# Four sequences through Mamba, attention, FFN and a routed FFN on one core: the input norms of sequences 2 and 3 start later, the prologue waits for one load at a time, and the first scan goes ahead of the first norm's scaling

## The reference, cut to what matters

```python
x = L0_attn_x                                    # (4, 512, 128)
x = x + _L0_attn_ref(_layernorm(x), ...)         # Mamba block, then attention and a gated FFN
x = x + _L0_ffn_ref(_layernorm(x), ...)          # ternary weights, gelu, layernorm
x = x + _L1_attn_ref(_layernorm(x), ...)         # second Mamba block
x = x + _L1_ffn_ref(_layernorm(x), ...)          # eight experts, the best one for each token
...
def mamba_block(x, ...):
    xz = rmsnorm(x, norm_m_w) @ in_proj_w.T
    x_ssm, z = jnp.split(xz, 2, axis=-1)
    x_ssm = silu(causal_conv(x_ssm, conv_w, 4 taps) + conv_b)
    Bp, Cp, dt_raw = split(x_ssm @ x_proj_w.T)
    delta = softplus(dt_raw @ dt_w.T + dt_b)
    # h = exp(delta * A) * h + delta * B * x ;  y = sum(h * C)   over 16 states
    y = selective_scan(x_ssm, delta, A, Bp, Cp, D_skip) * silu(z)
    return residual + y @ out_proj_w.T
```

## Time and profile before

| what | before |
|---|---|
| median of 3 runs, us | 734.0 (730.71 to 735.45) |
| profiled execution, us | 736.92 |
| its span, us | 735.1 |
| busy share of the span: PE, DVE, ACT, POOL | 81%, 80%, 67%, 57% |
| TensorE clock granted, mean | 0.919 of full |

### The profile page before, as it was taken

How to read it: one execution, slowest core, us unless ns; L and a number is a source line. 1 busy time by engine, 2 the same in 40 slices (tenths; PEclk the granted TensorE clock), 3 DMA queues, 4 the chain that set the end, 5 groups by cost and what they waited for, 6 DMA issues and landing times. The chain is left out here.

```text
span 735.1 us, 9892 instructions
## 1 busy us (share of the span) xinstructions
PE 596.1 (81%) x3364; PEld 395.2 (54%) x3364; DVE 587.0 (80%) x592; ACT 495.3 (67%) x921; POOL 420.3 (57%) x234
## 2 busy tenths in 40 slices
PE   6686686888988969998698996898677677869995
PEld 2154363456554545545454554554444466659995
DVE  3599989998989759987697889788899899854442
ACT  3859834877598786897878789678966678313231
POOL 0078754555666464735566346675687567445663
PEclk9689879798999889999899997899899899989999
DMA  4670650075005700007400075003800751257771
GB/s 133 261 238 15 238 223 1 0 282 195 25 4 193 284 0 2 1 2 290 186 1 0 1 266 210 1 0 101 361 1 1 263 199 53 67 162 236 220 228 42
DMA packets 35661, 91.63 MB, mean 125 GB/s; under 512 B 7492, under 2 KB 13115, under 8 KB 35611
## 3 DMA queue, kind: packets, MB, share of 16 engines
q1 hardware_dynamic: 34138, 87.93, 34.1%
q0 software_dynamic: 1472, 3.06, 1.5%
HBM read 87.87 MB, written 3.11 MB: 124 GB/s over the span
## 5 line engine op out<-in xcount | busy, mean ns | idle before, releaser
L527 POOL TENSOR_TENSOR hc<-hst,bc 128x1024 f32<-128x1024 f32 x127 | 299.0, 2362 | 164.6 <-DVE hst L1096 78.8
L1108 DVE TENSOR_TENSOR_SCAN hst<-dA,bank 128x1024 f32<-128x1024 f32 x84 | 191.4, 2282 | 2.1 <-PE bank L1760 0.2
L671 ACT ACTIVATE dA<-delta,m_A_s 128x511 f32<-128x511 f32 x256 | 173.2, 712 | 9.1 <-DVE hst L1108 6.0
L1470 PE MATMUL bank<-ident,hc 128*128 128x128 f32 x1016 | 142.8, 289 | 12.8 <-POOL hc L527 12.7
L1470 PEld LDWEIGHTS bank<-ident,hc 128*128 128x128 f32 x1016 | 125.3, 151 | 42.9 <-issue 24.0
L1079 DVE TENSOR_TENSOR bank<-bank,bc 128x1024 f32<-128x1024 f32 x79 | 97.1, 1229 | 10.0 <-DMA bc<-crows 3.7
L1377 PE MATMUL bank<-arena 128*32 128x128 f32 (+6 forms) x466 | 52.6, 361 | 11.9 <-ACT arena L761 6.5
L467 POOL TENSOR_TENSOR du<-delta,xs 128x512 f32<-128x512 f32 x15 | 19.1, 1273 | 71.5 <-DVE delta L1120 71.5
L1096 DVE TENSOR_TENSOR_SCAN hst<-dA,bank 128x512 f32<-128x512 f32 x44 | 53.7, 1220 | 1.5
L1090 DVE TENSOR_TENSOR_SCAN hst<-dA,bank 128x512 f32<-128x512 f32 x44 | 53.5, 1215 | 0.8
L1377 PEld LDWEIGHTS bank<-arena 128*32 128x32 f32 (+3 forms) x466 | 26.5, 141 | 38.9 <-issue 21.5
(11 more groups left out here) (262 smaller groups left out, 1092.8 us busy)
## 6 DMA issues: line engine op xcount, KB each, us to landing
bc<-crows SPq DMA_DIRECT2D x126, 512.0 KB, 9.3
bc<-in_w SPq DMA_DIRECT2D x23, 512.0 KB, 4.0
xin<-in_xT SPq DMA_DIRECT2D x8, 256.0 KB, 4.4
rows_out<-arena SPq DMA_DIRECT2D x1, 1056.0 KB, 6.4
conv<-in_m_cw SPq DMA_DIRECT2D x2, 512.0 KB, 4.5
crows<-prow SPq DMA_DIRECT2D x8, 64.0 KB, 1.6
arena<-rows_out,source POOLq DMA_INDIRECT x23, 3.5
out_rows<-zs,target POOLq DMA_INDIRECT x23
```

The lines of the kernel that those rows point to most:

```text
L527: pool.tensor_tensor(hc[:, g % HCRING], hst[:, g % HRING], bc[:, p, 1], ALU.mult) \
L671: act.activation(dA[:, g % RING, j, 1:], delta[:, h, 1:], ACT.Exp, scale=M[mamba_of(c)]["A"][:, h, n:n + 1]).then_inc(sems["dA"], 1)
L1108: dve.tensor_tensor_scan(hst[:, g % HRING].rearrange(flat), dA[:, g % RING].rearrange(flat), bank[:, first_bank:first_bank + 2, :].rearran ...
L1470: last = pe.matmul(bank[:, YB, P * j:P * j + P], hc[:, g % HCRING, n, P * j:P * j + P], ident[:], start=False, stop=s % PAIRS == PAIRS - 1 ...
```

## The change

Three things. In the **prologue**, `mean_d` gets a semaphore of its own, so that `n_center(0)` waits for the input and `center`, and only `n_variance(0)` for `mean_d`; the two copies of C rows on ScalarE go behind both decays of step 0; the root for the layernorm of sequence 0 moves into the loop (slot 0 of block 0) and the scaling of the z weights to slot 1, both behind the diagonal matrices. The **first scan**: `n_scaled` moves from slot 1 (ahead of `scan(0)`) to slot 3 (ahead of `scan(1)`). The **norms**: sequence 2 starts at slot 26 of block 0 (where sequence 3 was), sequence 3 at slot 34, which is slot 2 of block 1.

```diff
-NSTART = {1: 2, 2: 14, 3: 26}
+NSTART = {1: 2, 2: 26, 3: 34}
+N_SCALED = 3
+ROOT_AT = 0
+WZ_AT = 1
...
-            for dst, src in first:
-                sp.dma_start(dst, src).then_inc(sems["first_loaded"], 16)
+            sp.dma_start(center[:], d["center"]).then_inc(sems["first_loaded"], 16)
+            sp.dma_start(mean_d[:], d["mean_d"]).then_inc(sems["taps_in"], 16)
...
             def beside(b, t):
+                if b == 0 and t == ROOT_AT:
+                    inverse_root(bank[:, TB7, :], ht[:], eps_ln, "n_var", 1, "n_log", "n_rs")
+                if b == 0 and t == WZ_AT:
+                    act.activation(M[0]["wz"][:], M[0]["wz"][:], ACT.Copy, scale=norm_m[:]).then_inc(sems["scaled"], 1)
...
                     for k, at in NSTART.items():
-                        if b == 0:
-                            norm_ahead(k, t - at)
+                        norm_ahead(k, 32 * b + t - at)
...
                     decay(g, j)
-                    if g == 0:
+                if g == 0:
+                    for j in range(2):
                         act.wait_ge(sems["setup_pe"], 3 + j)
                         act.activation(bc[:, 0, 1, j], bank[:, (YB, FB5)[j], :], ACT.Copy).then_inc(sems["setup_act"], 1)
-            inverse_root(bank[:, TB7, :], ht[:], eps_ln, "n_var", 1, "n_log", "n_rs")
             act.wait_ge(sems["second_loaded"], 16 * len(second))
-            act.activation(M[0]["wz"][:], M[0]["wz"][:], ACT.Copy, scale=norm_m[:]).then_inc(sems["scaled"], 1)
             diagonal(0)
...
-                    if b == 0 and t == 1:
+                    if b == 0 and t == N_SCALED:
                         n_scaled()
...
-            pe.wait_ge(sems["first_loaded"], 16 * len(first))
+            pe.wait_ge(sems["first_loaded"], 16)
             n_center(0)
             warm(1)
+            pe.wait_ge(sems["taps_in"], 16)
             n_variance(0)
```

More of the change, by code:

```diff
@@ L339, in streams @@
                     yield "attention", i, a
-        first = [(dst[:], d[key]) for dst, key in ((center, "center"), (mean_d, "mean_d"))]
         def weights_of(m):
@@ L491, in weights @@
                     pool.wait_ge(sems["late_loaded"], 16 * len(late))
-                    pool.wait_ge(sems["taps_in"], 16)
+                    pool.wait_ge(sems["taps_in"], 32)
                     pool.tensor_tensor(conv[:], conv[:], winx1[:].unsqueeze(1).to_broadcast([P, TAPS, HALVES * P]),
@@ L499, in beside @@
                     for k, at in NSTART.items():
-                        if b == 0 and t == at + NAT["xn"]:
+                        if 32 * b + t == at + NAT["xn"]:
                             n_input(k)
@@ L1789, in beside @@
                     for k, at in NSTART.items():
-                        if b == 0 and t == at + NAT["cen"]:
+                        if 32 * b + t == at + NAT["cen"]:
                             n_center(k)
-                        if b == 0 and t == at + NAT["var"]:
+                        if 32 * b + t == at + NAT["var"]:
                             n_variance(k)
```

## The result

| | before | after |
|---|---|---|
| median of 20 runs each, us | 735.54 (730.71 to 741.54) | 738.91 (733.77 to 743.19) |
| profiled execution, span, us | 736.92, 735.1 | 738.95, 737.2 |
| TensorE clock granted, mean of that execution | 0.919 | 0.912 |

The ratio is 1.0055, 95% interval 1.0037 to 1.0074: the changed kernel is some 3 to 4 us slower, where 0.5 us less was forecast. That the median of 738.91 lies inside the stated range of 729 to 739, by 0.1 us, is luck: before itself came out at 735.54, where the three runs that the forecast had gave 734.0.

What follows compares the result with a forecast made beforehand. It took the prologue and ScalarE's queue to bound the first 36 us, block 1's preparation the rest of block 0. Terms -2.2 + 0 - 0.2 + 1.9 + 0 = -0.5 us took 734.0 to 733.5, range 729 to 739.

Steps and rivals of the forecast that it cites:

- The prologue: Start of the kernel: without mean_d in its wait, sequence 0's centring starts earlier, -2.2 us, bounds 0 and -2.25.
- the first rival: Prologue: center lands with mean_d, so nothing is gained there and block 1's added matmul costs; 736.0 us, chance 0.2.
- the third rival: Prologue: TensorE's clock rises too late for the earlier matmuls, up to 3.5 us more; 737.0 us, chance 0.1.
- ScalarE's order and the early scan: Block 0's start: second scan 1.65 us earlier, lost in later waits; 0 on the chain, bounds 0 and -1.65.
- The second rival: Block 0: VectorE's lead of 1.65 us reaches the end of the block; 731.9 us, chance 0.15.
- The third sequence's norm: Middle of block 0: sequence 2's norm leaves, only the y copy ahead of 64.84 profits; -0.2 us, bounds 0 and -0.5.
- SyncE: SyncE's queue: block 1's rows leave 3.3 us later, 1.5 us of cover left; 0, at most +1.
- the fourth rival: Head of block 1: SyncE's rows come late and the first drives wait, +1.5 us; 735 us, chance 0.05.
- The fourth sequence's norm at the head of block 1: Sequence 3's centring between accumulate(14) and accumulate(15) on the chain: +1.9 us, bounds +0.9 and +2.1; its variance matmul hidden.
- What is gained or lost before 98 us is then carried unchanged: Behind 98 us: no further gain or loss, as VectorE has no idle time from 97.53 through block 1's weight preparation.
- clock effects down the line that no row shows: Later blocks: named as what could move the time by over 1%, 7.3 us; no term in the sum.

Runs made afterwards that it cites:

- the two with the dummy: Kernel before plus one unread centring matmul between accumulate(14) and accumulate(15), compared twice against before: ratios 1.0050 and 1.0058.
- the one with the norms alone: Kernel before with only sequence 2's norm moved to slot 26 and sequence 3's to slot 34: 746.61 us, ratio 1.0069 against before.
- the two with the third norm back: Changed kernel with sequence 2's norm back at slot 14, sequence 3's at slot 34 or at 36: ratios 0.9993 and 1.0004 against before.
- the three comparisons: Changed kernel with all its parts against the kernel before, measured three times: ratios 1.0055, 1.0025 and 1.0013.
- half: Kernel before plus an unread 128x256 matmul between accumulate(14) and accumulate(15): 736.23 us, ratio 0.9957 against before.
- Before once more: Kernel before, unchanged, profiled a second time: span 732.0 us, 3.1 less than the profile that the forecast rests on.

## Why the prediction was wrong, by its own steps

**The prologue: over-sized by the one execution it was read from.** The load was right: `center` had landed by 3.7, so the first rival's condition, that it lands with `mean_d`, is false. Of the -2.2, the profiled pair shows 0.74 at the first decay (24.96 to 24.22), because the first projection ran at the low clock; that was the third rival, at about a third of its price of 3.5 us, and it happened in 2 of the 11 profiles with the own semaphore. The larger error is another. In the nine profiles of kernels with the common semaphore the centring began between 4.11 and 5.79, with a median of 4.58, with the own one between 3.41 and 3.88. The profile of before that I had was the latest of all. Medians of the first delta are 22.86 and 22.09, so the term is -0.8.

**ScalarE's order and the early scan: right, as far as the runs can tell.** 0 forecast, ratio 0.9998. VectorE waited 1.12 us for the softplus at 32.10, as the step had it. The second rival, that the lead of 1.65 us carries, is not borne out: from the first delta to the gate that kernel took 72.72 us, the two profiles of before 73.34 and 72.66. The interval of its ratio (0.9971 to 1.0025) by itself would allow it.

**The third sequence's norm: agrees in one pair, not shown.** The delta of block 1 moved by -0.93, which is the -0.74 that was left of the prologue and the -0.2 of this term. But from the first delta to that one the two profiles of before took 58.84 and 58.16 us, and the three of the changed kernel 58.66, 58.00 and 58.57, so 0.2 is under what these profiles can tell.

**SyncE: right.** The rows left 2.4 us later and released no drive; the fourth rival is false.

**The fourth sequence's norm at the head of block 1: right in place, wrong in price.** The matmul took the forecast 1.9 us in the chain, `n_variance(3)` was hidden (the residual at 104.98 had no wait), and the head grew by 0.8 to 1.1 in the seven profiles that have the whole matmul there, less than 1.9, since the clock rises behind it. The gate stood at 97.69, inside the 95.5 to 98.5 that the forecast allowed. At the end the same matmul costs 4.1 us against before (744.91 to 740.79) and 4.9 against the same matmul two slots later.

**The step that failed** is the last of the sum: "What is gained or lost before 98 us is then carried unchanged". Taken up to the gate, the measured terms cancel: -0.8 for the prologue and +0.8 to +1.1 for the head. The profiled pair says the same (+0.16 us at the gate, -0.36 at 174 us, +2.1 at the end). The loss comes behind 98 us, where the forecast had none. VectorE has indeed no idle time up to the weight preparation, but TensorE's clock down the line is not fixed: summed from the granted clocks of 5 us stretches it was at the low level for some 116 us in the profile of before and 126 in the changed one. The reading that fits best is that a shift by one microsecond moves the later idle times of TensorE against the clock's changes, and a stretch at the low level ends before or behind work that others wait for. With the whole matmul in the chain all seven profiles had the long follow-up (76.3 to 76.7 us), and the runs lean the same way: the clock was under 0.915 in 17 of 20 runs of the changed kernel (6 of 11 and 4 of 12 in its later comparisons, whose ratios were lower too) and in 9 of 9, 10 of 12 and 11 of 12 of the two with the dummy and the one with the norms alone, against 8 of 35, 12 of 29, 10 of 33, 5 of 32 and 4 of 23 for before in the five groups. A low clock alone does not make a kernel slow, though: the two with the third norm back had it in 9 of 12 and 9 of 11 runs, with ratios of 0.9993 and 1.0004. Within before's own runs a clock lower by 0.01 goes with 3 to 5 us more (lines through the runs of each group), so the 0.01 that separates 0.920 from 0.910 is of the size of what the head does not explain. That the clock is the cause and not a fellow of the longer time is argued from the matmuls themselves (1.90 against 2.92 to 3.63 us for one projection that others wait for) and not shown, since no run set the clock by hand. The forecast named "clock effects down the line that no row shows" and used them for the range alone, with no rival and no chance of their own.

**The sum, with measured terms:** -0.8 + 0 - 0.2 + 4.1 = +3.1 us, beside the +3.4, +1.5 and +1.9 of the three comparisons, as medians. The 4.1 is the price of the unread matmul in before and already holds what follows behind 98 us; with the third norm back the same place did not cost it, so the sum is near the first comparison and no proof. The forecast's own bounds add up to -3.5 and +3.6, where it has -3.4 and +3.5.

The Trainium skill (TensorE: Matmul & The Clock Gate, section on what's actually happening) says that the number of slow matmuls differs from run to run of one kernel and that the ramp costs less than 1% of a typical span. The first agrees with the two profiles of before, with 107 and 116 us at the low level. The second is said of the ramp; this kernel goes down and up all along, and the 20 runs of before spread over 1.5%.

**What stays open.** What decides between the two patterns was not found. It isn't the length in the chain (whole 1.0058, half 0.9957), nor the start of the block (the gate stood at 95.05 and 94.66 in good ones, at 94.64 in a poor one). Why the centring in the chain costs nothing when the third norm is back (0.9993), and why that norm's return gains nothing when the fourth is off the chain (1.0004 where 0.998 and less was expected), stays open; the parts of this change don't add up.

## What to carry to other kernels

A wait that one execution shows for a load is a sample: take its spread from a second profile of the same kernel before you sell the whole of it. Where TensorE goes between its two clock levels all the time, a matmul of 1.9 us put into the chain cost four and one of 1.06 gave three to four back, so a forecast from summed durations has to leave room of a few times its terms, with a chance for each side. Put a side task behind the last matmul that others wait for, not between two of them: two slots later the same norm cost nothing that could be measured. And judge such an edit by many runs: one program's profiles differed here by 2 us in one follow-up and by 2.7 us in one block.

## What the runs showed of the hardware

- Before once more against before: equal programs, spans 732.0 and 735.1 us, TensorE busy 591.7 and 596.1 us up to 730 us. The clock was at the low level for some 107 and 116 us of that time, summed from the granted clocks of 5 us stretches.
- Two loads of 64 KB, issued 0.47 us apart on one queue: the first released the centring between 3.41 and 3.88 in the eleven profiles where it stands alone, both together between 4.11 and 5.79 in nine.
- The same program, twice: 58.77 and 61.47 us from the first delta to the delta of block 1, with a granted clock of 1.00 and of 0.50 from 64 to 66 us.
- An added matmul of 1.06 us made the program 0.43% faster, one of 1.92 us in the same place made it 0.58% slower, and one of 1.02 us, 5 us later, changed nothing that the interval (0.9965 to 1.0021) would show.
